# A dense graph mix split by its keys: tiles 0 to 11 are mixed inside rounds 14 and 15, the rest in the last stage

## What is computed

```python
x = x + L0_gnn(layernorm(x), adj, ...)      # 4 heads of graph attention
x = x + L0_ffn(layernorm(x), ...)           # 8 heads, table lookup, causal attention
x = x + L1_gnn(layernorm(x), adj, H_v)
x = x + L1_ffn(layernorm(x), ...)
...
def L1_gnn(inputs, adj, H_v):
    scores = squeeze(inputs @ H_v)           # one number for each row
    mask = adj != 0.0
    logits = where(mask, adj * scores[None, :], -huge)
    m = max(logits, axis=1)                  # over all 2048 keys
    e = where(mask, exp(logits - m), 0)
    return (e / sum(e, axis=1)) @ inputs
```

## Time and profile before

| | us |
|---|---|
| median of 3 runs (lowest, highest) | 3279.63 (3275.05, 3288.53) |
| the profiled execution's own time | 3283.77 |
| its span, first to last instruction | 3282.0 |
| busy in the span: PE, DVE, ACT, POOL | 2180.5, 1779.5, 1041.6, 1995.3 |
| mean granted TensorE clock (share of full speed) | 0.799 |

### The profile page before, as it was taken

The page is one execution under the profiler, slowest core; times in us unless marked ns, Lnnn a source line. Parts: engine busy times, 40 slices in busy tenths (PEclk is TensorE's granted clock), DMA queues, the critical chain, the costliest instruction groups (busy, mean ns, idle before and its releaser), DMA issues.

```text
span 3282.0 us, 42226 instructions
## 1 busy us (share of the span) xinstructions
PE 2180.5 (66%) x14008; PEld 1507.6 (46%) x14066; DVE 1779.5 (54%) x6185; ACT 1041.6 (32%) x1966; POOL 1995.3 (61%) x2078
## 2 busy tenths in 40 slices
PE   5255555656666666767676868686867676856776
PEld 4134443434344444545454645554645454534555
DVE  3737373555547565656565746565646363125444
ACT  3133232323233333333333424342423232323333
POOL 0066766676676777777777777767677777740000
PEclk8677676677778787879887978897988787977888
DMA  2033433343343434343434343434343434341110
GB/s 58 15 103 96 132 109 114 107 119 115 96 139 91 139 109 139 109 139 110 139 110 136 108 132 106 137 103 122 95 120 109 126 103 124 109 121 68 58 58 20
DMA packets 164633, 348.21 MB, mean 106 GB/s; under 512 B 38816, under 2 KB 91712, under 8 KB 160192
## 3 DMA queue, kind: packets, MB, share of 16 engines
q0 software_dynamic: 98624, 269.62, 28.6%
q1 hardware_dynamic: 65792, 75.90, 7.2%
HBM read 333.83 MB, written 11.53 MB: 105 GB/s over the span
## 4 chain that ended last, share of the span: by engine, by line
PE 33%; DVE 25%; POOL 18%; issue 10%; ACT 8%; DVEq 3%; DMA 2%; SPq 0%; ACTq 0%; POOLq 0%
POOL ring L626 18%; PE acc L705 11%; PE turn L696 5%; PE wide L812 4%; DVE kv L1172 3%; PE rowsum L677 2%; DMA ring<-in_kv_table,idxT 2%; ACT att_p L962 2%; ACT pt_sb L910 2%; PE wide L756 2%; DVE att_m L1200 2%; DVE pos L1243 1%; DVE sims L1235 1%; PE wide L755 1%; DVE pos L1237 1%
## 5 line engine op out<-in xcount | busy, mean ns | idle before, releaser
L626 POOL DMA_INDIRECT ring<-in_kv_table,idxT x2048 | 1984.7, 969 | 927.2 <-issue 603.1
L705 PE MATMUL acc<-kv,pt_sb 128*128 128x128 f32 x3968 | 605.5, 306 | 111.0 <-ACT pt_sb L910 110.5
L705 PEld LDWEIGHTS acc<-kv,pt_sb 128*128 128x128 f32 x3968 | 548.8, 215 | 160.1 <-ACT pt_sb L910 160.1
L677 PE MATMUL rowsum<-ring,w_block 128*32 128x256 f32 x4096 | 342.2, 441 | 358.3 <-DMA ring<-in_kv_table,idxT 353.1
L910 ACT ACTIVATE pt_sb<-turn 128x512 f32<-128x512 f32 (+2 forms) x608 | 327.6, 562 | 411.1 <-PE turn L696 410.4
L812 PE MATMUL wide<-kv,qT 128*128 128x512 f32 (+3 forms) x576 | 279.9, 623 | 129.0 <-DVE gs L1172 88.2
L677 PEld LDWEIGHTS rowsum<-ring,w_block 128*32 128x32 f32 x4096 | 104.5, 117 | 560.6 <-DMA ring<-in_kv_table,idxT 400.1
L1200 DVE TENSOR_REDUCE att_m<-wide 128x1 f32<-128x128 f32 (+14 forms) x120 | 147.0, 1225 | 205.5 <-PE wide L812 200.1
L696 PE MATMUL turn<-ident,kv 128*128 128x128 f32 x1280 | 210.1, 304 | 64.7 <-ACT kv L386 24.5
L696 PE MATMUL turn<-ident,att_p 128*128 128x128 f32 x960 | 166.6, 310 | 110.1 <-ACT kv L924 98.0
L812 PEld LDWEIGHTS wide<-kv,qT 128*128 128x128 f32 x576 | 116.2, 219 | 267.7 <-issue 267.7
(11 more groups left out here) (228 smaller groups left out, 3184.5 us busy)
## 6 DMA issues: line engine op xcount, KB each, us to landing
kv<-in_adj SPq DMA_DIRECT2D x32, 1024.0 KB, 5.0
ring<-in_kv_table,idxT POOLq DMA_INDIRECT x2048
wq_pair<-in_Wq SPq DMA_DIRECT2D x64, 128.0 KB
v_dram<-sums_sb SPq DMA_DIRECT2D x128, 64.0 KB
kv<-v_dram SPq DMA_DIRECT2D x16, 512.0 KB, 4.1
att_p<-in_Wo SPq DMA_DIRECT2D x16, 512.0 KB, 5.5
xt<-in_x SPq DMA_DIRECT2D x16, 64.0 KB
x_dram<-x SPq DMA_DIRECT2D x16, 64.0 KB, 2.0
```

The costliest lines, as they stand in the source:

```text
L626: pool.indirect_dma_start(ring[:, slot, i, :], None, kv_table, bass.IndirectOffsetOnAxis(idxT[:, r % 3, u:u + 1], 0))\
L677: mm = pe.matmul(rowsum[32 * k:32 * k + 32, 0:ROW], w_block[:, at:at + 32], ring[:, slot, k, :], start=(tk == 0), stop=(tk == 3))
L705: mm = pe.matmul(dst, pt_sb[:, q % 2, b * P:(b + 1) * P], rhs(4 * q + b), start=(q + b == 0), stop=(q == len(widths) - 1 and b == widths[q ...
```

## The change

The keys of the mix are split. Tiles 0 to 11 ("far", 1536 keys) are final when round 11's tile is stored; their part of the mix is done for all 16 row tiles inside the steps of rounds 14 and 15, two row tiles a step (it["mix"]), with its own maximum and sum, and parked in DRAM (mix_dram). The keys of tiles 12 to 15 ("near", 512) follow in the tail, where both parts are merged in residual. The picks of tile 15 move from round 14 into round 13, which then has two picks a step, each second one as a step of its own; rounds 14 and 15 have none. Scores of the far keys are made in own of tile 13, those of tiles 12 to 14 at the end of step 3 of round 15. The near blocks of adj (16 loads) are issued by ACT in that step. The tail's stages M (mix), X (residual), R (route), H (hidden), Y (output) of the four groups stand in a written order, last_order, in place of one group after the other. The output is stored by SP in place of POOL. Many buffers move (sims, scratch, cand and others become parts of one tensor, pick).

```diff
+            mix = 8 * (n - (tiles - 2)) + 2 * s if n >= tiles - 2 else None
+            end = [1, 1, 1] if s == 3 else (0, 0, 0)
+            if n == tiles - 3:
+                k = 4 * (n + 1) + 2 * s
+                step([1, s > 0, 0], k=k, q=n, s=s)
+                left = step([0, 1, 0], k=k + 1, end=end, close=s < 3)
+            else:
+                left = step(counts[s], g=g if g < 4 * tiles else None, k=k if k < 4 * (tiles - 2) else None, q=n, s=s,
+                            end=end, close=s < 3, mix=mix)
             g += 1
...
+        FAR = LATE * P
+        far_adj = pick[:, 0:FAR]
+        far_score = pick[:, FAR:2 * FAR]
+        far_hide = pick[:, 2 * FAR:2 * FAR + FAR // 2].bitcast(BF16)
+        far_out = [w_tile, code_tile]
...
+        near = [kv[:, i, 0:512] if i < T - 1 else kv[:, 8, 1024:1536] for i in range(T)]
+        near_hide = [(kv[:, i, 512:768] if i < T - 1 else kv[:, 8, 1536:1792]).bitcast(BF16) for i in range(T)]
...
+        last_order = [("M", 0), ("M", 1), ("X", 0), ("R", 0), ("X", 1), ("H", 0), ("M", 2), ("Y", 0), ("R", 1), ("X", 2),
+                      ("H", 1), ("M", 3), ("Y", 1), ("R", 2), ("X", 3), ("H", 2), ("Y", 2), ("R", 3), ("H", 3), ("Y", 3)]
...
+            def mix(u):
+                def turns(j):
+                    i = 4 * u + j
+                    pe.wait_ge(mix_exp, i + 1)
+                    for b in range(4):
+                        mm = pe.transpose(turn[j % 2][:, b * P:(b + 1) * P], near[i][:, b * P:(b + 1) * P], ident[:, :])
+                    mm.then_inc(mix_turned, 1)
+                after(pe, hot_in, u - 1)
...
+            def mix(u):
+                act.wait_ge(mix_logit, u + 1)
                 for j in range(4):
                     i = 4 * u + j
-                    act.wait_ge(mix_logit, i + 1)
-                    act.activation(logit[:, j % 2, 0:N], logit[:, j % 2, 0:N], ACT.Exp, bias=mix_nm[:, j:j + 1],
-                                   accum_out=mix_sum[:, j:j + 1]).then_inc(mix_exp, 1)
-                    copy_chunks([4] * CH, mix_turned, mix_copied, i * CH)
+                    act.activation(near[i], near[i], ACT.Exp, bias=mix_nm[:, i:i + 1],
+                                   accum_out=mix_sum[:, i:i + 1]).then_inc(mix_exp, 1)
+                act.activation(mix_e[:, 4 * u:4 * u + 4], mix_d[:, 4 * u:4 * u + 4], ACT.Exp).then_inc(far_exp, 1)
...
+            def load_far(i):
+                if i == 0:
+                    sp.wait_ge(far_shown, 1)
+                after(sp, far_turned, len(chunk_widths(LATE)) * i)
+                sp.dma_start(far_adj, adj[i * P:(i + 1) * P, 0:FAR]).then_inc(far_adj_in, 16)
+            def store_far(i):
+                sp.wait_ge(far_taken, i + 1)
+                sp.dma_start(mix_dram[i * P:(i + 1) * P, :], far_out[i % 2][:, :]).then_inc(far_stored[i % 2], 16)
...
+                    if it["mix"] is not None:
+                        if it["mix"] > 0:
+                            store_far(it["mix"] - 1)
+                        load_far(it["mix"])
                     store_all(it)
+                    if it["mix"] is not None:
+                        load_far(it["mix"] + 1)
+                        store_far(it["mix"])
...
+                if d == T - 3:
+                    pe.wait_ge(far_rows, 1)
+                    for t in range(LATE):
+                        mm = pe.matmul(wide[:, t * P:(t + 1) * P], far_adj[:, t * P:(t + 1) * P], ident[:, :],
+                                       start=True, stop=True)
+                    mm.then_inc(far_shown, 1)
+                    pe.wait_ge(far_score_in, 1)
...
+            def sum_far(i):
+                pe.wait_ge(far_exp, i + 1)
+                widths = chunk_widths(LATE)
+                turn_and_sum(far_adj, widths, far_turned, far_copied, i * len(widths), lambda b: xn1T[:, b, :],
+                             acc[:, 2 * P:3 * P]).then_inc(far_summed, 1)
...
+                    if mix is not None:
+                        sum_far(mix)
+                        pe.wait_ge(far_taken, mix + 1)
                     pe.wait_ge(p_made, met(q, 2 * s) + 2)
                     values_of(2 * s + 1).then_inc(o_made, 1)
+                    if mix is not None:
+                        pe.wait_ge(o_in, met(q, 2 * s) // 2 + 1)
+                        sum_far(mix + 1)
                 if it["ahead"] is not None:
                     show_head(it["ahead"])
...
+                if q == T - 1 and s == STEPS - 1:
+                    act.wait_ge(o_made, met(q, 4) // 2)
+                    for u in range(T // 4):
+                        for i in range(4 * u, 4 * u + 4):
+                            act.dma_start(near[i], adj[i * P:(i + 1) * P, FAR:N]).then_inc(near_in[u], 16)
...
+                if mix is not None:
+                    exps(2 * s)
...
+            def exp_far(i):
+                act.wait_ge(far_logit, i + 1)
+                act.activation(far_adj, far_adj, ACT.Exp, bias=far_nm[:, i:i + 1],
+                               accum_out=far_sum[:, i:i + 1]).then_inc(far_exp, 1)
...
+            def far_logits(i):
+                dve.wait_ge(far_adj_in, 16 * (i + 1))
+                dve.wait_ge(far_score_in, 1)
+                dve.tensor_scalar(far_hide, far_adj, 0.0, HIDE, ALU.is_equal, ALU.mult)
+                dve.drain()
+                dve.tensor_tensor(far_adj, far_adj, far_score, ALU.mult)
+                dve.drain()
+                dve.tensor_tensor_reduce(far_adj, far_adj, far_hide, 1.0, -3e38, ALU.add, ALU.max, far_m[:, i:i + 1])
+                dve.drain()
+                dve.tensor_scalar(far_nm[:, i:i + 1], far_m[:, i:i + 1], -1.0, None, ALU.mult).then_inc(far_logit, 1)
...
+                if mix is not None:
+                    take_far(mix)
+                    far_logits(mix + 1)
...
+            def norm_tiles(lo, hi):
+                dve.wait_ge(x2_out, 16 * hi)
...
+            def show_scores(lo, hi, place):
+                place = place.rearrange("p (t n) -> p t n", n=P)
...
+                if d == T - 3:
+                    norm_tiles(0, LATE)
+                    show_scores(0, LATE, far_adj).then_inc(far_rows, 1)
+                if d == T - 1:
+                    for i in range(T):
+                        dve.wait_ge(near_in[i // 4], 64)
+                        dve.tensor_scalar(near_hide[i], near[i], 0.0, HIDE, ALU.is_equal, ALU.mult)
+                    dve.drain()
                 dve.wait_ge(own_p, 2 * d + 2)
...
+            def residual(u):
+                rows = slice(4 * u, 4 * u + 4)
+                dve.wait_ge(far_exp, T + u + 1)
+                dve.tensor_tensor(mix_r[:, rows], far_sum[:, rows], mix_e[:, rows], ALU.mult)
...
+            for stage, u in last_order:
+                if stage == "M":
+                    mix(u)
+                elif stage == "X":
+                    residual(u)
+                elif stage == "R":
+                    route(u)
+                elif stage == "H":
+                    hidden(u)
+                else:
+                    output(u)
```

More of the change, by code:

```diff
@@ L101, in build_network @@
     STEPS = 4
+    LATE = T - 4
     HW = P + 2 * GH
@@ L321, in tail_pool @@
+            for u in range(T // 4):
+                sp.wait_ge(moe_out, u + 1)
+                sp.dma_start(out.rearrange("(t p) d -> p t d", p=P)[:, 4 * u:4 * u + 4, :], y_moe[u % 2]).then_inc(t_out[u % 2], 16)
+            for b in range(2):
+                sp.wait_ge(t_out[b], 16 * (T // 8))
         def tail_pool(pool):
-            pool.wait_ge(picks_done, STEPS * T)
+            pool.wait_ge(far_summed, T)
             pool.memset(sel_expert, 0.0).then_inc(c_pool, 1)
@@ new lines, in output, with tail_vector, mix @@
+                after(act, t_out[u % 2], 16 * (u // 2))
+                act.activation(y_moe[u % 2], turn[1][:, :].rearrange("p (j n) -> p j n", j=4), ACT.Relu).then_inc(moe_relu, 1)
+            for stage, u in last_order:
+                if stage == "M":
+                    mix(u)
+                elif stage == "R":
+                    route(u)
+                elif stage == "H":
+                    hidden(u)
+                elif stage == "Y":
+                    output(u)
+        def tail_vector(dve, inverse_root, norm_tiles, show_scores):
+            norm_tiles(T - 1, T)
+            show_scores(T - 1, T, late[:, 0:P]).then_inc(near_rows, 1)
+            dve.wait_ge(near_score_in, 2)
+            def mix(u):
+                rows = slice(4 * u, 4 * u + 4)
+                for i in range(4 * u, 4 * u + 4):
+                    dve.tensor_tensor(near[i], near[i], near_score, ALU.mult)
@@ L717, in own_keys @@
                 mm.then_inc(own_s, 1)
+                if d == T - 1:
+                    pe.wait_ge(near_rows, 1)
+                    for b in range(3):
+                        mm = pe.matmul(turn[0][:, b * P:(b + 1) * P], late[:, b * P:(b + 1) * P], ident[:, :],
+                                       start=True, stop=True)
```

(13 more changed lines are left out.)

350 lines of the change are left out of this document (194 added, 156 removed).

## The result

The changed kernel takes 3329.56 us (median of 4 runs, 3324.45 to 3340.47), the kernel before 3280.13 on the same chip: ratio 1.0158, 95% interval 1.0126 to 1.0190. That is 49 us slower, where 3314 was forecast (+34) within 3270 to 3352. The profiled execution of after took 3324.45, its span is 3322.5. The spans differ by 40.5, the forecast for them was +38.

A forecast was written before the change was run, and what follows sets the result against it. Gathers (about 160 us a round) and an engine-to-engine chain in the tail bound the kernel. On 3282.0, +74, +36, +56 and -128 give 3320; less the profiled run's offset and 3 for overlaps, 3314 us, range 3270 to 3352.

The forecast's parts named there:

- Round 13, +74 forecast: Round 13: double-pick steps of 43.5 us, plus turned codes and norm and show of far tiles, add 74 us.
- My 5.1 for PE's part: Round 13: PE needs about 5.1 us for its next scores, with queries freed 5.8 before the second pick ends.
- two fifths: Round 13: the second picks were to make up two fifths of the +166 us up to the tail.
- Round 14, +36 forecast: Round 14: four steps of 40.7 us with two far tiles each, and 39.5 behind them, add 36 us.
- round 15, +56: Round 15: four steps of 41.5 us, 37.8 behind them, hiding masks and near loads add 56 us.
- The wait of 3.3 for the second far exponential: Rounds 14 and 15: of the second far tile's 11.1 us chain through one buffer, PE covers 7.9 and waits 3.3.
- The near loads: Round 15, step 3: the 16 near loads cost 5 us; a skill rule alone would give up to 20 more.
- The tail, -128 forecast: Tail: the new order shortens the chain without breaking it, 213 us for 341.4, so -128.
- Rival (a): Tail: it packs better, limited only by PE's own work, taking 160 us, the whole 3262; chance 1 in 10.
- Rival (b): Rounds 14 and 15: far tiles are cheap, without the 3.3 and 1.5 us; 38 less, 3276; chance 2 in 10.
- (c): Rounds 14 and 15: adjacency loads beside gathers are late, 3 us each; +45, 3360; chance 1 in 8.
- (d): Round 13: the second pick fits into DVE's waits, giving at most 4 x 5 us back; no separate chance given.

The follow-up runs named there:

- e11: The changed kernel with all work of the 16 far tiles left out, norm, show and merging kept: 3228.23 us, ratio 0.9841.
- e1: The changed kernel with the second pick of each step of round 13 left out, the first pick's codes used instead: 3283.39 us, ratio 1.000.
- e5: The changed kernel without the adjacency load for the second far tile of each step in rounds 14 and 15: 3298.48 us, ratio 1.0051.
- e6: The changed kernel with the 16 near loads issued by SP in steps 2 and 3 of round 15, not by ACT: 3330.70 us, ratio 1.0143.
- e2: The changed kernel with the tail's stages run one group after the other, same work: 3366.44 us, ratio 1.0261.
- e3: The changed kernel with the tail's stages cut finer and interleaved further, with more buffers: 3292.17 us, ratio 1.0027.
- e8: e3 with group 2's near logits ahead of the first normalisation, plus the edits of e6 and e7: 3273.01 us, ratio 0.9972.
- e7: The changed kernel with round 13's second-pick similarities made between the two heads' values: 3321.00 us, ratio 1.0117.
- e12: e10 with each step's second far load and first far store ahead of the value stores in SP's queue: 3253.55 us, ratio 0.9901.
- e9: The changed kernel with all far tiles in round 15, tile 15's picks back in round 14, steps reordered, near loads by SP: 3309.11 us, ratio 1.0084.
- e10: e9's rounds combined with the interleaved tail of e8: 3261.87 us, ratio 0.9947.

## Why the prediction was right

- **What bounds the kernel.** The gathers at 160 a round, hidden as soon as steps grow: shown by e11. That is why moving the picks out of round 14 brought back little. PE's wait for gathers remained in end and own (15.0 us in 4 waits in round 14).
- **Round 13, +74 forecast, +80.7 measured** (+78 with the 4 counted in the next round). Steps of 45.5 for 43.5: the copied sums (4.9), the second similarities (1.06 for 1.0) and the pick itself came as worked out; the assumption that PE's next scores are ready before was wrong by 1.8. PE came to them out of a wait of 8.5 us on the lower of its two clock levels. Its row behind the wait, then the stretch ahead of the wait and the one behind it (granted clock: third figure from the end):

```profile
2494.31 2.07 PE L915 MATMUL turn<-pick,xn1T 128*128 128x512 f32 x2 [8.51 <-ACT kv L1048]
```

```profile
2481.50:2485.00 3.50, 2.11 (x21) 0.65 (x19) 2.16 (x12) 0.98 (x2) 0.84 (x1) 1.00 0.00 0
2494.31:2498.18 3.87, 3.87 (x19) 1.10 (x19) 3.50 (x6) 0.76 (x2) 0.48 (x1) 0.50 0.11 34
```

The similarities and the pair took 3.9 us there, at a clock of 0.50; the same two groups took 2.1 at 1.00. My 5.1 for PE's part left no room for it. The step of the turned codes took 8.8 more (8), norm and show 14.7 (14.5), from 2668.05 to 2682.74 on DVE. DVE's busy time of 160.5 was forecast at 147; that figure was not part of the sum, and was too low.
- **What a second pick is worth** the sum did not tell. It adds 16.2 to the list of DVE's work, but taking it away gives back 12.9 (e1), since another wait stood behind it. So the mechanism was right, and the price as a difference would have been too high. The "two fifths" of +166 (68) that the prediction gave to the second picks were 51 of 177.
- **Round 14, +36 forecast, +38.0; round 15, +56 and +58.0.** Steps of 43.5, 41.3, 40.6 for 40.7 in round 14, and 42.7, 41.4 for 41.5 in round 15. The wait of 3.3 for the second far exponential measured 3.8 in the mean (15.3 in four), and e5 puts 3.5 a step on the load. The 1.5 taken for the lower clock behind that wait measured 1.2 in the step shown above. The first far tile, then the second, behind the wait:

```profile
2800.33:2805.30 4.97, 4.48 (x38) 4.05 (x36) 0.00 (x0) 2.56 (x5) 3.78 (x4) 1.00 0.47 104
2814.52:2820.69 6.17, 5.92 (x36) 5.68 (x37) 0.00 (x0) 1.68 (x3) 0.00 (x0) 0.72 0.07 23
```

That the two sums are so near has a share of luck. The first step of each round, from the tile's x2 to the second step's queries, was 3.8 and 5.9 longer than forecast; in round 15 PE waits 6.2 us there for one gather where before had 3.9. End and own of both rounds were shorter by 2.7 and 3.8, 36.8 and 36.4 us.
- **The near loads** were to cost 5: that step was some 3 longer. In e6 the extra time moved with the loads, which speaks for the transfers; no run leaves the loads out, so it stays open.
- **The tail, -128 forecast, -133.0.** Period 51.2 for 52.2; the first hidden layer ended 58 us into the tail, as forecast, and the end behind the third took 48 for 50. e2 shows that a quarter of the 133 is order.
- **Rival (a)** (the tail packs better) was rightly refused for this order: M2 ahead of Y0 holds it. e3 and e8 show that another order gets to 160, and that this alone nearly turns the sign (ratio 1.0027 in e3). That 160 was also the bound given there is luck: it was 140 of PE's work and 20 at the ends, and in e8 PE is busy for 120.4. **Rival (b)** is refuted by the waits, and by e5 and e11; **(c)** by the loads of the second far tiles, which are there 4.3 to 5.1 us behind their issue, where 4.3 was assumed and (c) asked for 3 more; **(d)** by the step of 45.5, and e7 shows that even made early the second pick finds only 13 us in a round.
- **The level.** 3314 for 3329.6: 2.5 of the 15.6 lie in the stretches, 3 in the overlaps that I took off and that did not come, the rest in the two profiled runs' distance to their medians. The 2.5 is again better than its parts: rounds 13 to 15 cost 11 more than forecast, the tail gave 5 more back, and round 13 began 3.2 earlier, which no edit explains.

## What to carry to other kernels

Work moved to "free" engine time is only free while a resource with a fixed rate (here 128 gathers a round) is longer than the step; work out the step with and without it, since removing from a step under that floor gives little (round 14 without its picks and without far tiles: 160.3 for 169.4) and adding beyond it costs in full. Here the same split of the keys lost 1.6% with the work spread over rounds 13 to 15, and won 1% once it stood in one round, in a better queue order and with a finer tail (e12). A single buffer that is loaded, worked on and emptied in turn has a period of its own (15.2 us), and its next load must stand in the queue directly behind what frees it: one store ahead of it cost 8 us in a step (e9 to e12). In a chain of stages over several groups, cut the stages so finely that no engine has to finish one group before it can start what the next group's critical stage needs.

## What the hardware showed unexpectedly

PE's time for the same work depends on the granted clock, and the clock fell behind PE's waits. The granted clock is a mean over spells at 1.2 and at 2.4 GHz, as a share of the higher level. The two pairs of rows in the section before show it on nearly the same work each: 1.00 ahead of a wait and 0.50 behind one of 8.5 us, 1.00 ahead and 0.72 behind one of 3.5 us. Over a whole stage, the tail's 642 rows took 148.5 us at a granted clock of 0.75 (e2), 142.1 at 0.78 (after), 129.8 at 0.84 (e12) and 121.2 at 0.86 to 0.89 (e3, e10). So 21 of the 42 us that the interleaved tail won are seen as PE's own busy time. But e12 and e10 run the same tail, at 0.84 and at 0.89, 8 us apart: the order alone does not fix the clock, and what made that difference was not looked for. The clock page of the Trainium skill (TensorE: Matmul & The Clock Gate, HAM oscillation) tells of a loop whose waits put PE back to the lower of its two levels each time; these rows agree with it.
